# Two-layer graph network: row halves for even and odd bodies in layer one, and in layer two one pick fewer and one gather more in one group of every fourth body

## The chip, the cores and the metric

The kernel runs on one core of one Trainium2 chip. The metric is the time of one execution on the device in microseconds (us), as the median of several executions. TensorE is called PE here (PEld is its weight load), VectorE DVE, ScalarE ACT, GpSimd POOL, SyncE SP.

## The reference, cut to what matters

Two layers of message passing over 6250 nodes with 64 features and 200,000 edges that are sorted by their target `dst`:

```python
# x: (6250, 64)   src, dst: (200000,)   edge_attr: (200000, 64)   edge_weight: (200000,)
h = maximum(layernorm(x), 0)
y = h @ W0 + b0                                            # layer one
agg = segment_sum(edge_weight[:, None] * y[src], dst, 6250)
deg = segment_sum(edge_weight, dst, 6250)
x = x + relu(agg / (deg[:, None] + 1e-6))

h = maximum(layernorm(x), 0)                               # layer two
m = gelu(concat([h[src], edge_attr]) @ W_msg + b_msg)
g = (1 + eps) * h + segment_sum(m, dst, 6250)
out = x + gelu(g @ W_upd + b_upd)
```

Each layer needs, for every edge, the row of a 6250 x 64 table at the edge's source, and adds up what it makes of it by the edge's target.

## The kernel before, in words

**Tiling.** The edges are cut into groups of 1024 (G = 128 x J, J = 8 tiles of 128 edges). There are 196 groups. Four groups (SLOTS = 4) make a body, so there are 49 bodies (BODIES) in each layer. Every engine has its own program, written out by hand in order, with loops (`Fori`) whose passes are bodies; the engines keep step by counting semaphores alone. There is no planner.

**Layer one.** Of the 8 tiles of a group, JA (4 or 5, by zone) are treated as products with small adjacency blocks on PE (`blocks_of`, L940; `adjacency_sums`, L959), and the other JH = J - JA (3 or 4) by gathered rows: POOL issues one indirect DMA per tile (`gathers`, L628 to L641) that fetches 128 rows of the table `h0_table` into `rows[:, slot, j, :]`, by the indices in `idx[:, slot, j]`. ACT's `weigh` (L764) waits for the rows of a slot, copies the next body's eight indices into `idx` (`copy_idx`, L670), and writes the weighted rows to `wrows` (L771), which counts up `s_used[slot]`. POOL gathers for the same slot of the next body only once that has happened. DVE builds the one-hot tiles (`build`, L1406 and L1408), and PE adds up by target in windows of 72 nodes (`window`, L1000). The five zones have different block shapes; the loops of a zone cover the bodies whose next two bodies lie in the same zone, and the bodies at a zone's edge are written out singly (`STRETCHES`). PE's loops of layer one are made with `hint_back_edge=True`.

**Between the layers** the sums are turned into the second table `p1_table`. `all_rounds` (on PE and DVE, ahead of the last body of layer one) holds the code for targets that lie too far apart; it is jumped over when there are none.

**Layer two.** Of the 8 tiles of a group, six (J0) are gathered from `p1_table` by POOL, and the last two (PICKS = 2) are "picked" on PE: the table lies in SBUF as `parts` (two parts of 7 x 448 columns), DVE compares the sources with the node number and makes a 0/1 matrix (`make_pick`, L1452), PE multiplies it with `parts` (`picks`, L917 to L934, the matmuls at L930: 2 tiles x 7 x 2 = 28 of 128x448 per group), and DVE masks out and adds up the right one of seven column blocks (`picked_rows`, L1469 and L1473) into `rows[:, slot, 6:8, :]`. PE also transposes the edge features (L1124), multiplies them by the lower half of W_msg (`edge_product`, L1135). DVE adds that product and the rows (`message_sum`, L1675; it waits for the slot's gathers, and counts up `s_used`), ACT applies the gelu (L860), and PE adds up by target in windows (L1000), two groups at a time; DVE adds these to the node sums (`sums`, L1490, and a small memset, L1510, that marks a group as done). If a group's targets span more than one window, `more_windows` (PE) and its counterpart in `sums` (DVE) do further ones; their code lies in the loop, and is jumped over otherwise.

PE's and DVE's order is one group ahead: in step s of a body, PE transposes and picks for group s + 1, then does the windows of groups s - 1 and s (for odd s), and then the product of group s + 1. The loops on PE, DVE, ACT and POOL run over 48 bodies, one body a pass, and the last body follows singly. PE's loop of layer two has no hint.

Of the kernel before, what the change touches and what calls it, by code (L numbers as in the profile page):

```python
# [7 lines left out]
class Zone:  # L8
# [43 lines left out]
    def gathered(self, b):  # L52
        return b * self.JH + (self.gathers_before - self.first * self.JH)


def two_layer_gnn(
# [97 lines left out]
    assert ZONES[-1].end == BODIES  # L154
    JA = max(z.JA for z in ZONES)
# [29 lines left out]
    GATHERED = ZONES[-1].gathered(BODIES)  # L185
    BANKS = (3, 5)
# [15 lines left out]
    with ctx:  # L202
# [235 lines left out]
        s_gat = [sem(f"gathered{s}") for s in range(SLOTS)]  # L438
# [24 lines left out]

        def unit(t, u):

            return t[:, u * KB:(u + 1) * KB, :]
# [10 lines left out]
        def _(sp):  # L477


            for one in (*s_used, s_prow, s_sumTc, s_sumc):  # L480
                sp.sem_inc(one, 1)
            sp.sem_inc(s_block, RING)
# [123 lines left out]
        @block.gpsimd  # L606
        def _(pool):
            nc.gpsimd.memset(ident[:, :], 0.0).then_inc(s_identf, 1)
            pool.wait_ge(s_identf, 1)
            nc.gpsimd.affine_select(out=ident[:, :], in_=ident[:, :], compare_op=ALU.not_equal, fill=1.0,  # L610
                                    base=0, pattern=[[-1, P]], channel_multiplier=1).then_inc(s_const, 1)
            nc.gpsimd.iota(iota_i[:, :], pattern=[[1, KH * P]], base=0, channel_multiplier=0).then_inc(s_const, 1)
            nc.gpsimd.memset(rows[:, :, :, D:DA], 1.0).then_inc(s_const, 1)
            nc.gpsimd.iota(node_i[:, :], pattern=[[0, 1]], base=0,
                           channel_multiplier=1).then_inc(s_const, 1)

            pool.wait_ge(s_src, 64)
            nc.gpsimd.tensor_copy(src_f[:, 0, :], src_raw[:, 0, :])
            nc.gpsimd.tensor_copy(src_f[0:HALF[1], 1, :], src_raw[0:HALF[1], 1, :]).then_inc(s_srcf, 1)
            pool.wait_ge(s_dst, 64)  # L620
            nc.gpsimd.tensor_copy(dst_f[:, 0, :], dst_raw[:, 0, :])
            nc.gpsimd.tensor_copy(dst_f[0:HALF[1], 1, :], dst_raw[0:HALF[1], 1, :]).then_inc(s_dstf, 1)
            nc.gpsimd.memset(sums_sb[:, :], 0.0).then_inc(s_zero, 1)
            for layer, table in ((0, h0_table), (1, p1_table)):
                if layer == 1:
                    pool.wait_ge(s_agg, UNITS)
                    nc.gpsimd.memset(sums_sb[D:DA, :], 0.0).then_inc(s_cleared, 1)
                pool.wait_ge(s_tabw[layer], (UNITS + 1) * 16)  # L628

# [13 lines left out]

                if layer == 0:
                    for z in ZONES:
                        with pool.Fori(z.first + 1, z.end + 1) as turn:
                            gathers(turn, range(z.JA, J))
                else:
                    with pool.Fori(BODIES + 1, 2 * BODIES) as turn:
                        gathers(turn, range(J0))  # L650
                    gathers(2 * BODIES, range(J0))

        @block.scalar
        def _(act):
# [53 lines left out]
            for s in range(SLOTS):  # L708
                copy_idx(s, s)
# [54 lines left out]
            def weigh(z, b, s, next_g):  # L764

                act.wait_ge(s_gat[s], z.gathered(b) * 16 + 16 * z.JH)
                copy_idx(next_g, s)
                act.wait_ge(s_dw[0], b * SLOTS + (s + 1))
                act.wait_ge(s_done, b * SLOTS + (s + 1))
                for j in range(z.JH):  # L770
                    last = nc.scalar.activation(wrows[s][:, j, :], rows[:, s, z.JA + j, :], ACT.Copy,  # L771
                                                scale=dw[:, s, 1, j:j + 1])
# [7 lines left out]
            def first(b, here, ahead, further):  # L780

                for s in range(2):
                    weigh(here, b, s, (b + 1) * SLOTS + s if ahead else s)
# [6 lines left out]
                for s in range(2, SLOTS):  # L790
                    weigh(here, b, s, (b + 1) * SLOTS + s if ahead else s)
# [61 lines left out]
            def message(b, s):  # L853
# [4 lines left out]
                act.wait_ge(s_used[s], b + (1 + BODIES + 1))  # L858
# [22 lines left out]
        def _(pe):  # L881
# [36 lines left out]
            def picks(b, q):  # L918
# [7 lines left out]
                for t in range(PICKS):  # L926
# [117 lines left out]
            def first(b, here, ahead, further):  # L1044
# [6 lines left out]
                for s in range(1, SLOTS, 2):  # L1051
# [6 lines left out]
                    for r in (s - 1, s):  # L1058
                        if not ahead and r == SLOTS - 1:
                            busy(28)  # L1060
                        pe.wait_ge(s_used[r], b + 2)
# [66 lines left out]
            def edge_product(b, s, shift):  # L1128
# [3 lines left out]
                if shift:  # L1132
                    pe.wait_ge(s_used[s], b + (1 + BODIES + 1))
# [10 lines left out]
            def second(b, last_body):  # L1144
                for s in range(SLOTS):
                    if not (last_body and s == SLOTS - 1):
                        edge_transpose(b, s, 1)
                        picks(b, s + 1)
# [32 lines left out]
        def _(dve):  # L1181
# [279 lines left out]
            def picked_rows(b, q):  # L1461
# [4 lines left out]
                dve.wait_ge(s_used[q % SLOTS], b + (BODIES + q // SLOTS + 1))  # L1466
                dve.wait_ge(s_prow, g + 1)
                of = mask[:, bass.ds(g, 1), :, :].rearrange("p g t a -> p (g t) a")
                nc.vector.tensor_tensor(sel[:, :, :, :],  # L1469
                                        ps[:, bank:bank + PICKS, 0:NA * D].rearrange("p t (a d) -> p t a d", d=D),  # L1470
                                        of.unsqueeze(3).to_broadcast([P, PICKS, NA, D]), ALU.mult).then_inc(s_sel, 1)
                dve.wait_ge(s_sel, g + 1)
                nc.vector.tensor_reduce(rows[:, q % SLOTS, J0:J, 0:D],  # L1473
                                        sel[:, :, :, :].rearrange("p t a d -> p t d a"),
# [191 lines left out]
            def message_sum(b, s, shift):  # L1666
# [4 lines left out]
                dve.wait_ge(s_gat[slot], 16 * GATHERED  # L1671
                            + (b + (s + shift) // SLOTS + 1) * (16 * J0))
# [9 lines left out]
            def second(b, last_body):  # L1682
                for s in range(SLOTS):
# [8 lines left out]
                    if not (last_body and s == SLOTS - 1):  # L1692
                        picked_rows(b, s + 1)
                        message_sum(b, s, 1)
# [45 lines left out]
```

## Time and profile before

| what | value |
|---|---|
| three runs | 2615.12, 2619.41, 2618.65 us, median 2618.65 |
| the profiled execution | 2620.69 us, its span 2618.9 us |
| PE busy | 2437.3 us (93%), 21749 matmuls |
| PEld busy | 2273.1 us (87%) |
| DVE busy | 2012.4 us (77%) |
| ACT busy | 1560.6 us (60%) |
| POOL busy | 1791.4 us (68%), 1879 instructions |
| layer one | from the start to about 1034 us |
| layer two's first picks | at 1077 us |

The span goes from the first to the last instruction. Each row of a timeline has the start, the duration, the engine, the line of the kernel, the operation with its operands, and in brackets the idle time of the engine just before it and what ended that ("issue": nothing that the profile shows). A busy PE is not PE at its peak, since the ends of matmuls are modelled. The share of a whole span is an average over two layers with different limits, so the windows of one stage say more than the page's first part.

### The profile page before, as it was taken

How to read it: one execution, taken by the hardware profiler on the slowest of the kernel's cores; microseconds unless marked ns; L12 is line 12 of the kernel's file. 1: busy time of each engine (PE TensorE's matmuls, PEld its weight loads, DVE VectorE, ACT ScalarE, POOL GpSimd, SP SyncE). 2: the span in 40 equal slices, each digit the busy share in tenths (PEclk: the TensorE clock that was granted, in tenths of full speed). 3: DMA queues.
4: the chain of work that ended last, by engine and by line, in shares of the span. 5: the costliest groups of instructions: out<-in, count | busy, mean ns of one | idle time of the engine just before them, and what ended most of it. 6: DMA issues, size and time to landing. Idle time of an engine off the chain costs nothing.

```text
span 2618.9 us, 70760 instructions
## 1 busy us (share of the span) xinstructions
PE 2437.3 (93%) x21749; PEld 2273.1 (87%) x21750; DVE 2012.4 (77%) x4216; ACT 1560.6 (60%) x5144; POOL 1791.4 (68%) x1879
## 2 busy tenths in 40 slices
PE   1588899999888888899999999999999999999998
PEld 1477799999888888899999999999999999999998
DVE  7888887766888886777777777777777777777774
ACT  2466666665666664566555656665656566556653
POOL 3377765677777773477777777777777777777771
PEclk9999999999999998899999999999999999999997
DMA  6111111111111110344444444445454544445451
GB/s 117 38 26 27 25 24 21 25 26 26 26 25 24 25 25 22 86 122 119 120 119 121 118 122 118 122 118 125 116 121 120 121 119 119 119 120 120 118 121 37
DMA packets 472280, 213.80 MB, mean 82 GB/s; under 512 B 264668, under 2 KB 441656, under 8 KB 472196
## 3 DMA queue, kind: packets, MB, share of 16 engines
q1 hardware_dynamic: 412548, 151.55, 22.1%
q0 software_dynamic: 59648, 61.20, 12.8%
q8 instruction: 45, 0.74, 0.1%
q14 instruction: 39, 0.32, 0.0%
HBM read 207.09 MB, written 5.51 MB: 81 GB/s over the span
## 4 chain that ended last, share of the span: by engine, by line
PE 58%; DVE 0%; ACT 0%; issue 0%; DVEq 0%
PE ps L930 43%; PE ps L1135 7%; PE ps L1000 4%; PE ps L1124 3%; PE ps L1082 1%; PE ps L1029 0%; DVE rows L1473 0%; DVE parts L1231 0%; DVE sel L1469 0%; DVE room L1675 0%; ACT h_sb L860 0%; DVE h_sb L1706 0%; DVE h_sb L1711 0%; ACT h_sb L878 0%; DVE tick L1510 0%
## 5 line engine op out<-in xcount | busy, mean ns | idle before, releaser
L639 POOL DMA_INDIRECT rows<-p_table,idx x1176 | 1109.8, 944 | 390.0 <-issue 342.8
L930 PE MATMUL ps<-parts,pick_all 128*128 128x448 f32 x5488 | 1162.0, 369 | 2.6 <-DVE parts L1231 2.6
L930 PEld LDWEIGHTS ps<-parts,pick_all 128*128 128x128 f32 x5488 | 1019.4, 189 | 77.7 <-issue 2.9
L639 POOL DMA_INDIRECT rows<-h_table,idx x688 | 665.3, 967 | 324.3 <-issue 200.9
L940 PE MATMUL ps<-hot_c,hot_p 128*128 128x150 f32 (+4 forms) x2336 | 435.0, 313 | 64.9 <-issue 37.1
L1469 DVE TENSOR_TENSOR sel<-ps,mask 128x896 f32<-128x896 f32 x196 | 214.0, 1092 | 307.0 <-PE ps L930 298.3
L940 PEld LDWEIGHTS ps<-hot_c,hot_p 128*128 128x128 f32 x2336 | 371.7, 192 | 85.7 <-issue 63.8
L731 ACT COPY adj<-ps 128x500 f32<-128x500 f32 (+4 forms) x880 | 349.9, 448 | 149.5 <-PE ps L940 136.9
L1452 DVE TENSOR_SCALAR pick_all<-src_all,node_f 128x1792 fp32r<-128x1792 int16 x196 | 406.5, 2074 | 27.4 <-issue 24.7
L1406 DVE TENSOR_SCALAR hot_p<-iota_p,scal 128x128 f32<-128x128 f32 (+2 forms) x880 | 301.1, 342 | 76.5 <-PE ps L940 56.0
L1473 DVE TENSOR_REDUCE rows<-sel 128x128 f32<-128x896 f32 x196 | 342.7, 1749 | 6.7
L1408 DVE TENSOR_SCALAR hot_c<-iota_c,scal 128x250 fp32r<-128x250 f32 (+4 forms) x880 | 340.8, 387 | 0.0
L860 ACT ACTIVATE h_sb<-room 128x512 f32<-128x512 f32 x98 | 62.0, 633 | 352.4 <-DVE room L1675 352.4
L959 PE MATMUL ps<-adj,h_sb 128*64 128x160 f32 (+4 forms) x4802 | 260.9, 267 | 1.9 <-ACT adj L731 0.9
L959 PEld LDWEIGHTS ps<-adj,h_sb 128*64 128x64 f32 x4802 | 250.4, 137 | 6.9 <-issue 2.0
L1000 PEld LDWEIGHTS ps<-onehot,room 128*65 128x65 f32 (+1 forms) x3336 | 175.1, 138 | 76.1 <-issue 59.0
L1000 PE MATMUL ps<-onehot,room 128*65 128x72 f32 (+1 forms) x3336 | 190.1, 229 | 50.8 <-DVE room L1447 41.9
L1135 PE MATMUL ps<-W1b_sb,eT 128*128 128x128 f32 x1568 | 216.6, 281 | 0.0
L1135 PEld LDWEIGHTS ps<-W1b_sb,eT 128*128 128x128 f32 x1568 | 197.5, 191 | 10.1
L860 ACT ACTIVATE room<-room 128x512 f32<-128x512 f32 x98 | 62.0, 632 | 240.8 <-DVE room L1675 240.8
L754 ACT ACTIVATE h_sb<-iota,dw 128x72 f32<-128x72 f32 x784 | 203.5, 345 | 0.0
L754 ACT ACTIVATE onehot<-iota,dw 128x72 f32<-128x72 f32 x784 | 203.3, 344 | 0.0
(182 smaller groups left out, 2345.0 us busy)
## 6 DMA issues: line engine op xcount, KB each, us to landing
src_all<-keys SPq DMA_DIRECT2D x196, 448.0 KB
ea<-in_edge_attr_dram SPq DMA_DIRECT2D x196, 256.0 KB
rows<-p_table,idx POOLq DMA_INDIRECT x1176
rows<-h_table,idx POOLq DMA_INDIRECT x688
x_sb<-in_x_dram SPq DMA_DIRECT2D x6, 224.0 KB, 4.3
h_table<-h_sb SPq DMA_DIRECT2D x6, 224.0 KB
p_table<-h_sb SPq DMA_DIRECT2D x6, 224.0 KB
out_dram<-h_sb SPq DMA_DIRECT2D x6, 224.0 KB
```

Source lines behind the costliest of these rows:

```text
L639: nc.gpsimd.indirect_dma_start(out=rows[:, s, j, 0:D], out_offset=None, in_=table[:, :], in_offset=bass.IndirectOffsetOnAxis(ap=idx[:, s, ...
L731: nc.scalar.copy(adj[:, 0:z.KH * z.KW, t * z.WT:(t + 1) * z.WT], psA[t % BANKS1][:, 0:z.KH * z.KW * z.WT].rearrange("p (k w) -> p k w", w= ...
L754: last = nc.scalar.activation(hots[s][:, j, :], iota[:, :], ACT.Abs, scale=-1.0, bias=dw[:, s, 0, j:j + 1])
L930: last = nc.tensor.matmul(to, hot[:, k, t * P:(t + 1) * P], parts[:, part, k, :, :].rearrange("p a d -> p (a d)"), start=(k == 0 and part ...
L940: last = nc.tensor.matmul(to[:, k * z.KW * z.WT:(k + 1) * z.KW * z.WT], one[:, k * P:(k + 1) * P], two[i], start=(i == 0), stop=(i == z.WP ...
L959: last = nc.tensor.matmul(psX[h:h + D, 0:z.cols], h_sb[:, n, :], adj[:, n, 0:z.cols], start=(n < 2), stop=(n >= NB - 2))
L1000: last = nc.tensor.matmul(psW[s % 2][at:at + width, :], lhs(j), hot[:, j, :], start=(j < sets), stop=(j >= n - sets))
L1135: last = nc.tensor.matmul(psM[:, q * P:(q + 1) * P], eT[:, q * P:(q + 1) * P], W1b_sb[:, :], start=True, stop=True)
L1406: nc.vector.tensor_scalar(one, iota_p[:, 0:z.KH * P], number(0), None, ALU.is_equal)
L1408: last = nc.vector.tensor_scalar(two[i], iota_c[:, 0:z.KW * z.WT], number(1), number(2 + i), ALU.is_equal, ALU.mult)
L1452: nc.vector.tensor_scalar(pick_all[:, q % 2, :].rearrange("p (k e) -> p k e", k=KA), src_bc[:, q % 2, :, 0:PICKS * P], node_f[:, 0:1], Non ...
L1473: nc.vector.tensor_reduce(rows[:, q % SLOTS, J0:J, 0:D], sel[:, :, :, :].rearrange("p t a d -> p t d a"), AX.X, ALU.add).then_inc(s_prow, 1)
```

## The change

In layer one each slot of `rows` and `idx` is used as two halves of four tiles (SET = 4), one for even and one for odd bodies, with semaphores `s_gat` of their own. POOL may then gather for a body as soon as the body two before it has been weighed (`s_used` starts at 2 instead of 1). ACT copies only the indices that are gathered, and for two bodies ahead; POOL's and ACT's loops of layer one make two bodies a pass.

In layer two the loops on POOL, PE and DVE make four bodies a pass (LOOP = 4), 12 passes instead of 48. In the last group (slot 3) of the fourth body, the first of the two picked tiles is gathered instead (`one_pick`): PE makes 14 of the 28 matmuls there, DVE masks and adds one tile instead of two, POOL issues seven gathers instead of six, and the count for which `message_sum` waits on that slot grows by one with each pass. ACT's loop of layer two stays at one body a pass.

```diff
+    def gathered_half(self, h):
+        return h * self.JH + (self.gathers_before // 2 - self.first // 2 * self.JH)
...
+    SET = J // 2
...
+    LOOP = 4
...
-        s_gat = [sem(f"gathered{s}") for s in range(SLOTS)]
+        s_gat = [[sem(f"gathered{p}_{s}") for s in range(SLOTS)] for p in range(2)]
...
+        def one_pick(phase, slot):
+
+            return phase == LOOP - 1 and slot == SLOTS - 1
...
+            for one in s_used:
+                sp.sem_inc(one, 2)
...
-                def gathers(turn, tiles):
+                def gathers(turn, free, tiles, p, phase=0):
                     for s in range(SLOTS):
                         pool.wait_ge(s_const, CONSTS)
                         pool.wait_ge(s_idx[s], turn)
 
-                        pool.wait_ge(s_used[s], turn)
+                        pool.wait_ge(s_used[s], free)
                         if s == 0:
                             pool.sem_inc(s_passed, 1)
-                        for j in tiles:
+                        for j in range(tiles.start, tiles.stop + one_pick(phase, s)):
                             nc.gpsimd.indirect_dma_start(
...
-                            ).then_inc(s_gat[s], 16)
+                            ).then_inc(s_gat[p][s], 16)
+
+                def half_gathers(z, b, p):
+                    gathers(b + 1, b + 1, range(p * SET, p * SET + z.JH), p)
 
                 if layer == 0:
                     for z in ZONES:
-                        with pool.Fori(z.first + 1, z.end + 1) as turn:
-                            gathers(turn, range(z.JA, J))
+                        with pool.Fori(z.first // 2, z.end // 2) as h:
+                            for p in range(2):
+                                half_gathers(z, 2 * h + p, p)
+                        if z.end % 2:
+                            half_gathers(z, z.end - 1, 0)
                 else:
-                    with pool.Fori(BODIES + 1, 2 * BODIES) as turn:
-                        gathers(turn, range(J0))
-                    gathers(2 * BODIES, range(J0))
+                    with pool.Fori(0, (BODIES - 1) // LOOP) as i:
+                        for phase in range(LOOP):
+                            turn = i * LOOP + (BODIES + 1 + phase)
+                            gathers(turn, turn + 1, range(J0), 0, phase)
+                    gathers(2 * BODIES, 2 * BODIES + 1, range(J0), 0)
...
+            def copy_half_idx(z, b, p, s):
+                nc.scalar.copy(idx[:, s, p * SET:p * SET + z.JH].unsqueeze(2),
+                               src_tab[:, z.JA:J, bass.ds(b * SLOTS + s, 1)]).then_inc(s_idx[s], 1)
...
-            for s in range(SLOTS):
-                copy_idx(s, s)
+            for p in range(2):
+                for s in range(SLOTS):
+                    copy_half_idx(ZONES[0], p, p, s)
...
-            def weigh(z, b, s, next_g):
-
-                act.wait_ge(s_gat[s], z.gathered(b) * 16 + 16 * z.JH)
-                copy_idx(next_g, s)
+            def weigh(z, b, h, p, s, ahead, further):
+
+                act.wait_ge(s_gat[p][s], z.gathered_half(h) * 16 + 16 * z.JH)
+                if further:
+                    copy_half_idx(further, b + 2, p, s)
+                elif not ahead:
+                    copy_idx(s, s)
...
-                    with act.Fori(start, end) as b:
-                        first(b, *zones)
-                else:
-                    first(start, *zones)
+                    with act.Fori(start // 2, end // 2) as h:
+                        for p in range(2):
+                            first(2 * h + p, h, p, *zones)
+                if (end - start) % 2:
+                    first(end - 1, (end - 1) // 2, (end - 1) % 2, *zones)
...
-                for t in range(PICKS):
+                for t in range(one_pick(phase, q), PICKS):
                     to = ps[:, BANKS[q % 2] + t, 0:NA * D]
...
-            with pe.Fori(0, BODIES - 1) as b:
-                second(b, False)
-            second(BODIES - 1, True)
+            with pe.Fori(0, (BODIES - 1) // LOOP) as i:
+                for phase in range(LOOP):
+                    second(i * LOOP + phase, phase, False)
+            second(BODIES - 1, 0, True)
...
+                own = slice(int(one_pick(phase, q)), PICKS)
+                n = PICKS - own.start
+                of = mask[:, bass.ds(g, 1), own, :].rearrange("p g t a -> p (g t) a")
...
-                dve.wait_ge(s_gat[slot], 16 * GATHERED
-                            + (b + (s + shift) // SLOTS + 1) * (16 * J0))
+                landed = 16 * GATHERED + (b + (s + shift) // SLOTS + 1) * (16 * J0)
+                if slot == SLOTS - 1:
+
+                    landed = landed + (i + one_pick(phase, slot)) * 16
+                dve.wait_ge(s_gat[0][slot], landed)
...
-            with dve.Fori(0, BODIES - 1) as b:
-                second(b, False)
-            second(BODIES - 1, True)
+            with dve.Fori(0, (BODIES - 1) // LOOP) as i:
+                for phase in range(LOOP):
+                    second(i * LOOP + phase, phase, False, i)
+            second(BODIES - 1, 0, True, (BODIES - 1) // LOOP)
```

## Rows read from the trace of the kernel before

**Rows 1.** The page's chain that ended last, share of the span by engine.
```profile
PE 58%; DVE 0%; ACT 0%; issue 0%; DVEq 0%
```

**Rows 2.** Windows, layer two: length, busy us (instructions) by engine, granted PE clock, DMA.
```profile
1200.00:2500.00 1300.00, 1300.00 (x9500) 1201.45 (x9499) 979.52 (x1015) 786.51 (x2283) 970.87 (x1030) 1.00 0.49 120
```

**Rows 3.** Chain of waits, layer two: start, us, what; two picks, two groups apart.
```profile
1516.90 5.67 PE ps L930 x28
...
1532.25 5.67 PE ps L930 x28
```

**Rows 4.** Timeline of POOL, layer two: first, 12th, 18th, 606th and last gather.
```profile
1078.43 0.95 POOL L639 DMA_INDIRECT rows<-p_table,idx  x1 [14.88 <-issue]
...
1092.17 0.94 POOL L639 DMA_INDIRECT rows<-p_table,idx  x1 [0.30 <-issue]
...
1099.66 0.94 POOL L639 DMA_INDIRECT rows<-p_table,idx  x1 [0.30 <-issue]
...
1833.74 0.94 POOL L639 DMA_INDIRECT rows<-p_table,idx  x1 [0.30 <-DVE room L1675]
...
2562.41 0.95 POOL L639 DMA_INDIRECT rows<-p_table,idx  x1 [0.30 <-issue]
```

**Rows 5.** L639: one wait of POOL before it (us, times); who waited for it.
```profile
  ACT room L771: 123.4, 52
...
  DVE room L1675: 2.3, 1
```

**Rows 6.** Timeline of DVE, layer two: message sums, and a body's end and next start.
```profile
1096.07 0.69 DVE L1675 TENSOR_TENSOR room<-ps,rows 128x512 f32<-128x512 f32 x1
...
1105.13 0.69 DVE L1675 TENSOR_TENSOR room<-ps,rows 128x512 f32<-128x512 f32 x1 [2.30 <-DMA rows<-p_table,idx]
...
1518.79 0.06 DVE L1510 MEMSET tick<- 1x1 f32 x1
1519.37 2.08 DVE L1452 TENSOR_SCALAR pick_all<-src_all,node_f 128x1792 fp32r<-128x1792 int16 x1 [0.52 <-issue]
...
2584.56 0.69 DVE L1675 TENSOR_TENSOR room<-ps,rows 128x512 f32<-128x512 f32 x1 [0.20 <-DVE rows L1473]
```

**Rows 7.** The page's queues that fetch instructions: packets, MB, share of 16 engines.
```profile
q8 instruction: 45, 0.74, 0.1%
q14 instruction: 39, 0.32, 0.0%
```

**Rows 8.** Timelines of PE and DVE, layer one: idle times without a semaphore, and 661.49.
```profile
632.70 3.65 PE L940 MATMUL ps<-hot_c,hot_p 128*128 128x200 f32 x12 [2.39 <-issue]
...
661.49 1.47 PE L1000 MATMUL ps<-onehot,room 128*65 128x72 f32 x20 [2.74 <-DVE room L1447]
...
997.30 0.37 PE L940 MATMUL ps<-hot_c,hot_p 128*128 128x250 f32 x1 [2.85 <-issue]
...
1014.60 0.53 DVE L1400 TENSOR_TENSOR onehot<-iota,dw 128x360 f32<-128x360 f32 x1 [3.98 <-issue]
...
1021.26 0.28 PE L970 MATMUL ps<-eye,xs 128*40 128x64 f32 x2 [3.61 <-issue]
```

**Rows 9.** Timeline of PE around the jump from one body of layer two to the next.
```profile
1514.16 1.22 PE L1000 MATMUL ps<-h_sb 128*64 128x72 f32 x32
1515.31 1.16 PE L1135 MATMUL ps<-W1b_sb,eT 128*128 128x128 f32 x8
...
1516.66 5.92 PE L930 MATMUL ps<-parts,pick_all 128*128 128x448 f32 x28
...
1523.66 5.92 PE L930 MATMUL ps<-parts,pick_all 128*128 128x448 f32 x28
```

**Rows 10.** Windows around three of the idle times of rows 8; the clock is third last.
```profile
632.00:640.00 8.00, 7.30 (x46) 7.01 (x46) 4.38 (x14) 3.06 (x7) 5.71 (x6) 0.79 0.14 29
661.00:669.00 8.00, 6.88 (x72) 6.43 (x72) 7.24 (x25) 5.50 (x20) 5.79 (x7) 1.00 0.12 23
997.00:1001.00 4.00, 3.69 (x19) 3.51 (x20) 2.58 (x9) 1.86 (x4) 3.05 (x4) 0.57 0.15 31
```

More of the change, by code:

```diff
@@ L154, in two_layer_gnn @@
     assert ZONES[-1].end == BODIES
+    SET = J // 2
+    assert all(z.JH <= SET and z.first % 2 == 0 and z.gathers_before % 2 == 0 for z in ZONES)
     JA = max(z.JA for z in ZONES)
@@ L184, in two_layer_gnn @@
     J0 = J - PICKS
-    GATHERED = ZONES[-1].gathered(BODIES)
-    BANKS = (3, 5)
+    LOOP = 4
+    assert (BODIES - 1) % LOOP == 0
+    GATHERED = ZONES[-1].gathered_half((BODIES + 1) // 2)
     BANKS = (3, 5)
@@ L477, in _ @@
         def _(sp):
-            for one in (*s_used, s_prow, s_sumTc, s_sumc):
+            for one in (s_prow, s_sumTc, s_sumc):
                 sp.sem_inc(one, 1)
+            for one in s_used:
+                sp.sem_inc(one, 2)
             sp.sem_inc(s_block, RING)
@@ L770, in weigh @@
                 for j in range(z.JH):
-                    last = nc.scalar.activation(wrows[s][:, j, :], rows[:, s, z.JA + j, :], ACT.Copy,
+                    last = nc.scalar.activation(wrows[s][:, j, :], rows[:, s, p * SET + j, :], ACT.Copy,
                                                 scale=dw[:, s, 1, j:j + 1])
@@ L778, in next_dw, with first @@
                 copy_dw(0, b * SLOTS + s, s % SLOTS, z)
-            def first(b, here, ahead, further):
+            def first(b, h, p, here, ahead, further):
                 for s in range(2):
-                    weigh(here, b, s, (b + 1) * SLOTS + s if ahead else s)
+                    weigh(here, b, h, p, s, ahead, further)
                 for s in range(2, SLOTS):
@@ L790, in first @@
                 for s in range(2, SLOTS):
-                    weigh(here, b, s, (b + 1) * SLOTS + s if ahead else s)
+                    weigh(here, b, h, p, s, ahead, further)
                     if ahead:
@@ L916, in _, with picks @@
                 turn(w_raw, half, psR[half])
-            def picks(b, q):
+            def picks(b, q, phase=0):
                 hot = pick_all[:, q % 2, :].rearrange("p (k e) -> p k e", k=KA)
@@ L1142, in _, with second @@
             edge_product(0, 0, 0)
-            def second(b, last_body):
+            def second(b, phase, last_body):
                 for s in range(SLOTS):
@@ L1147, in second @@
                         edge_transpose(b, s, 1)
-                        picks(b, s + 1)
+                        picks(b, s + 1, phase)
                     last_group = last_body and s == SLOTS - 1
@@ L1459, in next_pick, with picked_rows @@
                 make_pick(b, q)
-            def picked_rows(b, q):
+            def picked_rows(b, q, phase=0):
                 g = b * SLOTS + q
@@ L1465, in picked_rows @@
                 dve.wait_ge(s_picked, g + 1)
-                dve.wait_ge(s_used[q % SLOTS], b + (BODIES + q // SLOTS + 1))
+                dve.wait_ge(s_used[q % SLOTS], b + (BODIES + q // SLOTS + 2))
                 dve.wait_ge(s_prow, g + 1)
[L1468 to L1471, printed above, removed]
+                own = slice(int(one_pick(phase, q)), PICKS)
+                n = PICKS - own.start
+                of = mask[:, bass.ds(g, 1), own, :].rearrange("p g t a -> p (g t) a")
+                nc.vector.tensor_tensor(sel[:, own, :, :],
+                                        ps[:, bank + own.start:bank + PICKS, 0:NA * D].rearrange(
+                                            "p t (a d) -> p t a d", d=D),
+                                        of.unsqueeze(3).to_broadcast([P, n, NA, D]), ALU.mult).then_inc(s_sel, 1)
                 dve.wait_ge(s_sel, g + 1)
-                nc.vector.tensor_reduce(rows[:, q % SLOTS, J0:J, 0:D],
-                                        sel[:, :, :, :].rearrange("p t a d -> p t d a"),
+                nc.vector.tensor_reduce(rows[:, q % SLOTS, J0 + own.start:J, 0:D],
+                                        sel[:, own, :, :].rearrange("p t a d -> p t d a"),
                                         AX.X, ALU.add).then_inc(s_prow, 1)
@@ L1680, in _, with second @@
             message_sum(0, 0, 0)
-            def second(b, last_body):
+            def second(b, phase, last_body, i):
                 for s in range(SLOTS):
@@ L1692, in second @@
                     if not (last_body and s == SLOTS - 1):
-                        picked_rows(b, s + 1)
-                        message_sum(b, s, 1)
+                        picked_rows(b, s + 1, phase)
+                        message_sum(b, s, 1, phase, i)
                     if s % 2:
```

8 lines of the change are left out of this document (4 added, 4 removed).

## The prediction

> **What bounds the kernel now.** I read the page's chain of waits first: PE alone holds 58% of the span in it and no other engine a whole per cent [rows 1]. The windows then say where: from 1200 to 2500 us PE is busy 1300.00 of 1300.00 us, DVE 980, POOL 971, ACT 787, at a granted clock of 1.00 [rows 2]. So layer two is a pure PE chain, and what comes off PE there comes off the end, as long as nothing else steps into its place. The pieces of that chain are the picks: 28 matmuls in 5.67 us, and every two groups take 15.35 us (1516.90 to 1532.25) [rows 3], so a body of four takes 30.70.
>
> The page's busy share (POOL 68%) misleads about what stands next. From 1078.43 to 1833.74 POOL issues 606 gathers back to back, one in 755.31 / 605 = 1.248 us (0.94 busy and 0.30 between) [rows 4]. A body's 24 take 29.96 us, so POOL is only 0.74 us a body faster than PE. It starts late and needs some 25 bodies to catch up; only then does it wait for free slots.
>
> Layer one is another matter: POOL waits 123.4 us there for ACT's weighing, but nothing waits for a gather of layer one; the one engine held up by a gather is DVE, once, 2.3 us, in layer two [rows 5].
>
> **The change part by part.** The profiled execution took 2620.69 us with a span of 2618.9; the median of the three runs is 2618.65, 2.04 less. I work out differences on the profiled one and put them on the median.
>
> *Halves of the slots in layer one.* It removes waits of POOL (a gather for body b+1 no longer needs body b weighed). Since no engine waits for those gathers [rows 5], I take 0. It costs four more index copies ahead of the loops, where ACT goes on to wait for DVE's and PE's tables (that wait hides them; without it, under a microsecond), and 12 gathers earlier there; bound: a microsecond or two either way. ACT's loops become two bodies long. No new instruction stands on PE.
>
> *One pick fewer.* 14 matmuls at 5.67 / 28 = 0.2025 us are 2.84 us [rows 3], in 12 groups: 34.0 us off PE's chain. DVE's multiply and sum of these groups halve; DVE has 320 us to spare in the 1300 [rows 2], so that is worth nothing.
>
> *One gather more.* 12 x 1.248 = 15.0 us more on POOL. Per four bodies POOL needs 97 x 1.248 = 121.1 us, PE 4 x 30.70 - 2.84 = 119.9: POOL would be the slower one by 1.2 us a pass and never catch up. The end that POOL allows: the last of 1188 gathers ends at 1078.43 + 1187 x 1.2485 + 0.95 = 2561.3. From there to landing, two rows bound it: the message sum at 1105.13 waited for a gather issued by 1100.60 (4.53 us), the one at 1096.07 did not wait on one issued by 1093.11 (at most 2.96) [rows 4, 6]. So the last message sum, now at 2584.56 [rows 6], can't come before 2564.3 to 2565.8: of the 34.0 us no more than 18.8 to 20.3, say 19.5, can be had. What follows that sum stays as it is. Behind the added gather stand only POOL's own next gathers, and the first to be held up by them is that message sum.
>
> The Trainium skill (DMA: Bandwidth & Descriptors, Anatomy of one DMA, SWDGE path) gives about 2.0 us of fixed cost to such a transfer; the row with 4.53 us disagrees for at least one gather, and by the page's figure the cap would be an estimated 21.3 us.
>
> *Four bodies of code in one pass.* This is the part I give most weight. PE's and DVE's loops of layer two now hold four bodies, and PE's loop has no hint for its jump back. A pass today runs 9500 matmuls and 9499 weight loads in 1300 us, about 448 records in 30.70 us, and PE never stalls at the jump [rows 2]. The instruction queues fetched 45 and 39 packets in the whole span [rows 7]; one packet per pass of this loop would already be 48. So one body's code stays at hand. Whether four bodies' code does, no row shows. What code that is not at hand costs, rows do show, as idle time with no semaphore behind it ("issue"): at the first matmuls after a loop of layer one is left, 2.39 us (632.70) and 2.85 us (997.30); after the jump over the further rounds, PE 3.61 us (1021.26) and DVE 3.98 us (1014.60), where DVE's usual gap at a jump back is 0.52 (1519.37) [rows 6, 8].
>
> There are 12 passes, so 11 jumps back. Bounds of the price on PE: 0 and 3.61 us each. I take (2.39 + 2.85) / 2 = 2.62, the rows that stand at a loop's end on PE. At the jump back PE has little queued: after the last product of a body (1515.31 to 1516.47) come the next transposes and picks (1516.66) [rows 9].
>
> A stall of that size can also bring PE's granted clock from its upper level (2.4 GHz) to its lower (1.2): around the 2.39 us idle the granted clock of 8 us was 0.79 (lost 0.21 x 8 = 1.7 us), around the 2.85 us idle that of 4 us 0.57 (0.43 x 4 = 1.7 us), but around an idle of 2.74 us 1.00 (nothing) [rows 8, 10]. I take two passes of three at 1.7 us: 1.1 us a pass. Bounds: 0 and 1.7. Nothing hides either: PE is the chain [rows 1, 2].
>
> DVE's own jump: 3.98 - 0.52 = 3.46 us later, its pick would be ready at 1521.45 + 3.46 = 1524.91, and PE wants it at 1523.66 [rows 6, 9]: 1.25 us late if PE is on time, nothing if PE itself stalls 2.62. So it does not add.
>
> *Sum.* -34.0 + 11 x (2.62 + 1.13) = -34.0 + 41.3 = +7.3 us. POOL's cap does not bind: a pass of PE is 123.7 us against POOL's 121.1. 2618.65 + 7.3 = 2626.
>
> The Trainium skill (Runtime: NRT & Kernel Launch, Instruction fetch mechanics) says that code is held in blocks of 256 instructions, 2048 of them on PE and 512 on the others, that straight code is fetched ahead, and that a taken branch to code outside the window waits for the fetch. Its other sentence, of only two such blocks, the trace contradicts for PE: 448 records, the skipped branch's products (another 32 matmuls and as many loads a group pair, by the row at 1514.16 [rows 9]) and the waits are more than 512, and no pass stalls. By the 2048, one body fits, and four, at least 4 x (448 + 128) = 2304 by my estimate, do not, so the stall would come in every pass.
>
> **Rivals.**
> 1. *No stall at the jump back; POOL becomes the bound* (the other side: faster). The four bodies stay at hand, or the queue covers the fetch. For it: 48 jumps back today without a stall; against it: code four times as long as any shown to be kept. PE would end 34.0 us earlier, POOL allows 19.5: 2599. It holds as long as the stall is under (34.0 - 19.5) / 11 = 1.3 us a pass; a stall of DVE alone (1.25 us) ends here too.
> 2. *Stall, but the clock holds.* For it: the 2.74 us idle; against it the two others. -34.0 + 11 x 2.62 = -5.2: 2613.
> 3. *Stall at its upper row, clock down each time.* 11 x (3.61 + 1.7) = 58.4, less 34.0: +24.4, 2643. For it: the far jump's 3.61 is also a taken branch, while the loop ends are not.
> 4. *The earlier gathers of layer one matter.* No engine waits for them; a microsecond or two, inside every range.
>
> **How the numbers follow.** A measurement of this kernel tells 0.2%, 5.2 us, from no change. Forecast case 0.52, own range 2617 (2.39 a pass and the clock down in one of three: 11 x 2.96 - 34.0 = -1.4) to 2635 (2.85 and down in all: 11 x 4.55 - 34.0 = +16.1); rival 1 0.28; rival 2 0.10; rival 3 0.10. Faster: 0.28, half of rival 2 (0.05) and 0.03 of the forecast: 0.36. Same: the other half of rival 2 and 0.17 of the forecast: 0.22. Slower: 0.32 of the forecast and rival 3: 0.42. The range for 8 in 10 has to reach rival 1 and rival 3: 2598 to 2645.
>
> **What would show it.** In the windows, PE's busy time in layer two: 100% less 2.6 us every 122 us or so if I am right, with 11 idle times marked "issue" ahead of the transposes (L1124), a granted clock under 1.00 there, and some hundred more instruction packets. Rival 1 shows the packets nearly unchanged or the idle under 1.3 us, POOL back to back (1.248 us) until the end, and DVE's message sum waiting for gathers. Picks: 12 groups with 14 matmuls in 2.84 us; L930 falls from 5488 to 5320. POOL's layer-one wait for L771 should shrink while layer one ends where it does. I am wrong if PE's idle at the passes is small, if layer one's end moves by more than 3 us, or if a gather takes another time than 1.248 us.

## The result and the profile after

The changed kernel takes 2653.6 us (median of 4 runs), the kernel before in the same comparison 2616.9: a ratio of 1.0157, 95% interval 1.0124 to 1.019. It is slower by about 1.6%, where the prediction said 2626 (+7.3 us) with a range up to 2645. The profiled execution has a span of 2657.3 us, 38.4 more than the one before.

Where the 38.4 lie, the first and last picks of layer two say. In the timeline of PE of the kernel before they are:

```profile
1077.46 8.37 PE L930 MATMUL ps<-parts,pick_all 128*128 128x448 f32 x28 [2.64 <-DVE parts L1231]
...
2575.58 5.92 PE L930 MATMUL ps<-parts,pick_all 128*128 128x448 f32 x28
```

and in that of the changed kernel (the picks' line is now L959):

```profile
1075.67 7.98 PE L959 MATMUL ps<-parts,pick_all 128*128 128x448 f32 x28 [2.19 <-DVE parts L1261]
...
2613.96 5.92 PE L959 MATMUL ps<-parts,pick_all 128*128 128x448 f32 x28
```

From the start of the first to the end of the last, layer two took 2581.50 - 1077.46 = 1504.04 us before and 2619.88 - 1075.67 = 1544.21 after: +40.2, with 168 matmuls fewer. Layer one and the way into layer two took 1.8 us less, the tail the same (37.4 us each). The 1.8 is chance as far as the traces show: the twelve kernels of the experiments have the layer one of the changed kernel, and there the first picks start anywhere from 1070.7 to 1082.7. I call this stretch "layer two" below and compare kernels by it; the three kernels with all picks in which PE never stands there agree within 1 us (1503.2 to 1504.2).

The window that stood in [rows 2], the instruction queues of [rows 7], and PE's and DVE's waits in layer two, all of the changed kernel:

```profile
1200.00:2500.00 1300.00, 1250.23 (x9024) 1149.59 (x9023) 931.53 (x983) 762.21 (x2214) 949.61 (x1007) 0.98 0.49 118
```

```profile
q8 instruction: 184, 3.01, 0.5%
q14 instruction: 124, 1.02, 0.1%
```

```profile
PE ps L1153 <- issue: 48.4, 11, 6.2
...
DVE pick_all L1482 <- issue: 37.6, 22, 3.5
...
DVE room L1711 <- DMA rows<-p_table,idx: 10.6, 4, 5.1
```

PE was never idle in this window before; now it is for 50 us of it, and over all of layer two it stands 48.4 us at 11 places, all ahead of the transposes that open a pass (L1153, the old L1124), with no semaphore to blame. The instruction packets on q8 rose from 45 to 184: (184 - 45) / 11 = 12.6 a jump at most, since the first pass through the longer code has its packets in the 184 too.

One such place, in the timelines of PE and then of DVE of the changed kernel; the brackets hold the idle time before the row and what ended it:

```profile
1448.17 3.08 PE L959 MATMUL ps<-parts,pick_all 128*128 128x448 f32 x14
1451.09 1.05 PE L1164 MATMUL ps<-W1b_sb,eT 128*128 128x128 f32 x8
1451.98 0.60 PE L1153 MATMUL ps<-ident,ea 128*128 128x128 f32 x4
1452.68 6.04 PE L959 MATMUL ps<-parts,pick_all 128*128 128x448 f32 x28
...
1459.80 1.16 PE L1164 MATMUL ps<-W1b_sb,eT 128*128 128x128 f32 x8
1465.43 0.72 PE L1153 MATMUL ps<-ident,ea 128*128 128x128 f32 x4 [4.47 <-issue]
1465.84 7.49 PE L959 MATMUL ps<-parts,pick_all 128*128 128x448 f32 x28
1473.17 1.05 PE L1164 MATMUL ps<-W1b_sb,eT 128*128 128x128 f32 x8
1474.06 0.60 PE L1153 MATMUL ps<-ident,ea 128*128 128x128 f32 x4
1474.41 5.92 PE L959 MATMUL ps<-parts,pick_all 128*128 128x448 f32 x28
```

```profile
1450.55 2.08 DVE L1482 TENSOR_SCALAR pick_all<-src_all,node_f 128x1792 fp32r<-128x1792 int16 x1
...
1463.22 0.06 DVE L1543 MEMSET tick<- 1x1 f32 x1
1466.53 2.08 DVE L1482 TENSOR_SCALAR pick_all<-src_all,node_f 128x1792 fp32r<-128x1792 int16 x1 [3.26 <-issue]
```

Three losses are to be read here. PE stands 4.47 us at the jump. Its next 28 picks, from the transposes' start to the product's (1465.43 to 1473.17), take 7.74 us. Undisturbed it is 5.95 from the end of one product to the next (1516.47 [rows 9] to 1522.42 in the kernel before, below, where the transposes start 0.16 us before that end). Of the 1.79 us more, 0.16 is this lost overlap and the rest the clock. And after the thinner group (14 matmuls, 1448.17) the next picks begin 0.70 us after their transposes (1451.98, 1452.68), where 0.35 is usual (1474.06, 1474.41), because DVE made the pick for them only from 1450.55 to 1452.63. That recurs behind all 12 thinner groups. The two rows of the kernel before:

```profile
1516.31 0.60 PE L1124 MATMUL ps<-ident,ea 128*128 128x128 f32 x4
...
1522.42 1.05 PE L1135 MATMUL ps<-W1b_sb,eT 128*128 128x128 f32 x8
```

The windows of the changed kernel show the clock (third column from the right):

```profile
1461.00:1465.00 4.00, 0.00 (x0) 1.00 0.23 35
1465.00:1469.00 4.00, 3.57 (x13) 0.61 0.45 96
1469.00:1473.00 4.00, 4.00 (x21) 0.96 0.52 147
1473.00:1477.00 4.00, 4.00 (x27) 1.00 0.34 76
```

### The profile page after: what moved, and what is told of

Its sections match the earlier page's. It is cut to its first block, busy times and chain, and to the rows that moved or that the text cites. A ratio compares the mean times of both kernels' runs of the same rounds, so it can differ in the third digit from the quotient of the medians.

```text
span 2657.3 us, 69927 instructions
## 1 busy us (share of the span) xinstructions
PE 2427.3 (91%) x21581; PEld 2258.4 (85%) x21582; DVE 1993.3 (75%) x4216; ACT 1560.9 (59%) x5144; POOL 1805.8 (68%) x1891
## 4 chain that ended last, share of the span: by engine, by line
PE 66%; DVE 18%; issue 8%; POOL 3%; DVEq 3%; DMA 1%; ACT 1%; SPq 0%; POOLq 0%; ACTq 0%
PE ps L959 37%; PE ps L969 8%; PE ps L1029 6%; PE ps L1164 6%; PE ps L988 5%; DVE hot_c L1438 5%; DVE hot_p L1436 4%; POOL rows L651 3%; PE ps L1153 3%; DVE hot_lo L1438 2%; DVEq L1515 1%; DVE pick_all L1482 1%; PE ps L1111 1%; DVE rows L1506 1%; DVE sums_sb L1523 1%
## 5 line engine op out<-in xcount | busy, mean ns | idle before, releaser
L959 PE MATMUL ps<-parts,pick_all 128*128 128x448 f32 x5320 | 1144.4, 373 | 3.5 <-DVE parts L1261 2.2
L959 PEld LDWEIGHTS ps<-parts,pick_all 128*128 128x128 f32 x5320 | 1001.2, 191 | 82.0 <-DVE pick_all L1482 4.1
L1501 DVE TENSOR_TENSOR sel<-ps,mask 128x896 f32<-128x896 f32 x196 | 208.2, 1062 | 335.3 <-PE ps L959 327.0
L1482 DVE TENSOR_SCALAR pick_all<-src_all,node_f 128x1792 fp32r<-128x1792 int16 x196 | 406.5, 2074 | 43.8 <-issue 37.6
L1506 DVE TENSOR_REDUCE rows<-sel 128x128 f32<-128x896 f32 x196 | 332.1, 1695 | 6.7
```

Of the source, the lines that this page charges most:

```text
L959: last = nc.tensor.matmul(to, hot[:, k, t * P:(t + 1) * P], parts[:, part, k, :, :].rearrange("p a d -> p (a d)"), start=(k == 0 and part ...
L1482: nc.vector.tensor_scalar(pick_all[:, q % 2, :].rearrange("p (k e) -> p k e", k=KA), src_bc[:, q % 2, :, 0:PICKS * P], node_f[:, 0:1], Non ...
L1506: nc.vector.tensor_reduce(rows[:, q % SLOTS, J0 + own.start:J, 0:D], sel[:, own, :, :].rearrange("p t a d -> p t d a"), AX.X, ALU.add).the ...
```

## The experiments

My theory F: PE's loop of four bodies is more code than stays at hand, so that PE waits at every jump back and then runs at the lower clock. Rival D: PE's gap is a wait for DVE, which stands at its own jump. Rival P: the thinner groups and added gathers cost the time. Layer two lasts, in us, with PE's idle at the jumps and the ratio of the whole time to the kernel before:

| kernel | layer two | PE's idle, waits | ratio (95%) |
| --- | --- | --- | --- |
| before | 1504.0 | 0 | 1 |
| changed | 1544.2 | 48.4, 11 for code | 1.0157 (1.0124 to 1.019) |
| halves alone | 1503.2 | 0 | 0.9986 (0.9961 to 1.0011) |
| four bodies of code, no thinner group | 1581.6 | 50.2, 11 for code | 1.0263 (1.0214 to 1.0312) |
| four on PE alone | 1580.9 | 50.0, 11 for code | 1.0268 (1.0219 to 1.0318) |
| four on DVE alone | 1510.7 | 2.9, 9 for picks | 1.0000 (0.998 to 1.0019) |
| three bodies of code | 1571.4 | 45.4, 15 for code | 1.0225 (1.0186 to 1.0263) |
| two bodies of code | 1530.0 | 19.5, 23 for picks | 1.0102 (1.0061 to 1.0143) |
| two on PE alone | 1504.2 | 0 | 1.0009 (0.9987 to 1.0031) |
| changed, hint on PE | 1516.9 | 29.8, 11 for code | 1.0075 (1.0046 to 1.0105) |
| nest of four | 1493.6 | 13.2, 11 for picks | 0.9961 (0.9937 to 0.9986) |
| nest of six | 1496.8 | 8.1, 7 for picks | 0.9956 (0.9932 to 0.998) |
| nest of four, hint on DVE | 1483.3 | 0.4, 1 for a pick | 0.9942 (0.9921 to 0.9962) |
| nest of six, hint on DVE | 1488.4 | 0 | 0.9972 (0.9954 to 0.999) |

### The parts of the change alone

Halves alone. All picks are put back and the loops of layer two hold one body:

```diff
-            return phase == LOOP - 1 and slot == SLOTS - 1
+            return False
...
-            with pe.Fori(0, (BODIES - 1) // LOOP) as i:
+            with pe.Fori(0, (BODIES - 1) // 1) as i:
```

(the loops of DVE and POOL likewise; with no thinner group, `message_sum` no longer adds the passes to its count).

> Layer one's halves alone: loops of one body in layer two, all picks put back. Both theories: no stall on PE, 2615 us (layer two begins 1.8 us earlier than in the kernel before: 1075.67 against 1077.46), instruction packets on q8 about 45. If the halves themselves cost something in layer two (by an earlier state of POOL or by ACT's longer code), over 2620.

2604.97 us against 2609.28 in its comparison: no difference that can be told, and PE is busy through the window again:

```profile
1200.00:2500.00 1300.00, 1300.00 (x9499) 1200.60 (x9498) 977.51 (x1018) 789.11 (x2293) 972.85 (x1030) 1.00 0.50 120
```

Four bodies of code with all picks put back:

```diff
-            return phase == LOOP - 1 and slot == SLOTS - 1
+            return False
```

(`message_sum` is changed as above)

> The changed kernel with all picks put back (28 matmuls in each group, 24 gathers a body), loops of four bodies kept. Theory F: the loss stands alone, 2617 - 1.8 (layer two begins that much earlier) + 11 x (4.4 + 1.8) = 2683 us, slower than the changed kernel. Rival P (the added gathers and the thinner groups cost the time, the idle is only where it shows): about 2615, as before.

2682.31 us. The expected 2683 came from F's prices in the changed kernel, and P fell: without a thinner group or an added gather the kernel is slower still.

Four bodies on PE alone, against the kernel just named:

```diff
-            with dve.Fori(0, (BODIES - 1) // LOOP) as i:
+            with dve.Fori(0, (BODIES - 1) // 1) as i:
...
-                    with pool.Fori(0, (BODIES - 1) // LOOP) as i:
+                    with pool.Fori(0, (BODIES - 1) // 1) as i:
```

> As the kernel with halves alone, but PE's loop of layer two holds four bodies; DVE's and POOL's hold one. Theory F: all of the loss is PE's own, 2683 us, PE's idle 4.4 us at 11 jumps though DVE never stands at its own; q8 about 184 packets, q14 as before. Theory D: 2615.

2683.21 us. The page's queues and the wait, with DVE's packets back at the 44 of the halves alone:

```profile
q8 instruction: 184, 3.01, 0.5%
q14 instruction: 44, 0.36, 0.0%
```

```profile
PE ps L1153 <- issue: 50.0, 11, 5.1
```

DVE did not stand at its jumps here, and PE's idle is the same: D is out, the loss is PE's own code. Layer two is 77.7 us longer than with the halves alone, 50.0 of it idle and 26.5 the slower picks behind the 11 jumps (counted as above, with 0.16 a jump of lost overlap).

Four bodies on DVE alone, against the same kernel of four bodies:

```diff
-            with pe.Fori(0, (BODIES - 1) // LOOP) as i:
+            with pe.Fori(0, (BODIES - 1) // 1) as i:
...
-                    with pool.Fori(0, (BODIES - 1) // LOOP) as i:
+                    with pool.Fori(0, (BODIES - 1) // 1) as i:
```

> As the kernel with halves alone, but only DVE's loop of layer two holds four bodies; PE's and POOL's hold one. DVE alone is to pay: about 3.5 us idle at 11 jumps, its pick then some 0.9 to 1.2 us late for PE (as in the loops of two, 19.5 us in 23 waits), 11 x 1.0 = 10 to 13 us: ratio to the kernel before about 1.003 to 1.005, q8 45 packets, q14 about 44 + 11 x 7.3 = 124. If DVE's stall is hidden when PE is on time, 1.000.

The ratio says no difference; the profile says 7.5 us more in layer two than with the halves alone (0.7 a jump, 11 jumps), less than expected:

```profile
q14 instruction: 124, 1.02, 0.1%
```

```profile
PE ps L959 <- DVE pick_all L1482: 2.9, 9, 0.5
```

Only q14 rose here (q8 stays at 45), and only q8 with four bodies on PE alone: q8 carries PE's code, q14 DVE's.

### How much code stays at hand

Loops of three bodies, of two, and of two on PE alone with one on DVE and POOL, all without a thinner group; on PE

```diff
-            with pe.Fori(0, (BODIES - 1) // LOOP) as i:
-                for phase in range(LOOP):
-                    second(i * LOOP + phase, phase, False)
+            with pe.Fori(0, (BODIES - 1) // 3) as i:
+                for phase in range(3):
+                    second(i * 3 + phase, phase, False)
```

(and with 2 for 3):

> As the kernel with halves alone, loops of three bodies: 9.5 packets of PE's code a pass, 15 jumps. Theory F1 with the amount below 9.5 packets: 15 x (4.55 + 2.2) = +100, 2707 us, q8 about 45 + 15 x 9.5 = 185. F1 with the amount above it: 2605 to 2609, q8 near 45. A partial loss (only the blocks that do not fit are fetched anew) would lie between, with fewer than 185 packets.

> As the kernel with halves alone (all picks put back), but the loops of layer two hold two bodies on PE, DVE and POOL. In the loop of four PE took (184 - 45) / 11 = 12.6 instruction packets a pass, about 3.2 a body. Theory F1 (PE keeps a fixed amount of code; a loop within it is fetched once, one beyond it is fetched anew in every pass): two bodies are 6.3 packets; if that is within the amount, no idle at the jumps, q8 near 45 packets, 2605 to 2609 us. Theory F2 (any loop much longer than one body is fetched anew): 23 jumps x (4.4 + 1.8) = +143, 2750 us.

> As the kernel with halves alone, but only PE's loop holds two bodies. If what the loops of two cost (19.5 us of PE waiting for DVE's pick) is all DVE's, this costs nothing: ratio 0.998 to 1.001, q8 47 packets, q14 44, no wait of PE. If PE's longer code costs by itself, some 20 us, 1.008.

Three bodies: 2673.5 us. PE fetches (94 - 45) / 15 = 3.3 packets a jump at most and stands 3.03 us at each. That is the partial loss which the expectation named last, not the full refetch.

```profile
q8 instruction: 94, 1.54, 0.2%
```

```profile
PE ps L1153 <- issue: 45.4, 15, 3.4
```

Two bodies: PE's packets stay at 47 and it never waits for code, but it waits for DVE's pick, which is late because DVE now stands at its jump; the time is 2638.1 us against 2618.2. Neither theory had said so. The page's queues, PE's wait, and one of DVE's jumps:

```profile
q14 instruction: 160, 1.31, 0.2%
q8 instruction: 47, 0.77, 0.1%
```

```profile
PE ps L959 <- DVE pick_all L1482: 19.5, 23, 1.2
```

```profile
1337.51 2.08 DVE L1482 TENSOR_SCALAR pick_all<-src_all,node_f 128x1792 fp32r<-128x1792 int16 x1 [3.66 <-issue]
```

With two on PE alone (q8 47, q14 44) layer two lasts 1504.2: on PE two bodies are free, and the two-body cost was DVE's.

The 3.2 packets a body in these expectations (6.3 for two, 9.5 for three) are too many. A kernel with a loop of two has one more copy of the body than one with a loop of one, and where nothing is fetched again q8 rises by it from 45 to 47 (the nests below, with as many copies, have 47 too): 2 packets a copy, under 3 in any case. With 2 each for the added copies the refetches are (94 - 49) / 15 = 3.0 a jump for three bodies and (184 - 51) / 11 = 12.1 for four, which is as much as all four bodies or more.

### Undoing the stall

The hint for the jump back, which PE's loops of layer one have, on PE's loop of layer two in the changed kernel:

```diff
-            with pe.Fori(0, (BODIES - 1) // LOOP) as i:
+            with nc.Fori(0, (BODIES - 1) // LOOP, engines=(mybir.EngineType.PE,), hint_back_edge=True) as i:
```

> The changed kernel whole; the one edit is the hint for the jump back on PE's loop of layer two (the same hint that PE's loop of layer one has). Theory F (PE waits at each of its 11 jumps for its own code, 4.40 us, and then runs at the lower clock, 1.8 us): if the hint has the loop's first code there in time, both go, 11 x 6.2 = 68 us less on PE, and POOL becomes the bound: 2597 us, up to 2610 if DVE's own idle at its jump (3.3 us) now shows by 1.25 us each time; PE's idle ahead of the transposes under 1 us. If the hint brings only the loop's first block and the rest is still fetched late, the idle shrinks to half, about 2625. Theory D (PE's gap is a wait for DVE, which stands 3.3 us at its own jump): nothing changes, 2653, since DVE has no hint.

2631.61 us against 2609.28: still slower than before, near the middle case (2625). Layer two is 27.3 us shorter than in the changed kernel: 18.6 of idle, 9.1 of slower picks. The page's packets and PE's wait:

```profile
q8 instruction: 174, 2.85, 0.5%
```

```profile
PE ps L1153 <- issue: 29.8, 11, 3.8
```

The packets fell by about one a jump, and the idle time from 4.41 to 2.71 us. That fits a hint that brings only the start of the loop early, while the rest is still fetched anew; the trace does not show which packet is which.

The nest keeps the work of the change with two bodies of code: an inner loop makes one body three times, and the fourth, with the thinner group, is written out behind it (on DVE and POOL as on PE; the nest of six has 6 for 4):

```diff
-            with pe.Fori(0, (BODIES - 1) // LOOP) as i:
-                for phase in range(LOOP):
-                    second(i * LOOP + phase, phase, False)
+            with pe.Fori(0, (BODIES - 1) // 4) as i:
+                with pe.Fori(0, 4 - 1) as k:
+                    second(i * 4 + k, 0, False)
+                second(i * 4 + (4 - 1), LOOP - 1, False)
```

> The work of the changed kernel (halves, one pick fewer and one gather more in every fourth body), but each pass of four is an inner loop of one body, three times, and a fourth body written out: two bodies of code on PE, DVE and POOL. Theory F1 with room for two bodies: no stall on PE, 12 x (2.84 - 0.35) = 29.9 us off PE, POOL (97 gathers of 1.248 us a pass, 121.1 us) is the bound; the cap of the prediction, 19 to 21 us below the kernel before: 2588 to 2590. If leaving the inner loop and entering it again stalls as leaving a loop did in layer one (2.4 to 2.85 us), the 12 exits cost 29 to 34 us and nothing is gained: about 2610.

> The same nest with the thinner group in every sixth body, 8 in all. PE: 8 x (2.84 - 0.35) = 19.9 us less; POOL: 145 gathers, 181.0 us a pass against PE's 181.7, so POOL's cap (24.5 us) does not bind: 2588 us by F1 with room for two bodies, no better than the nest of four, but with POOL off the path.

Both beat the kernel before: 2607.2 and 2600.6 us against 2618.2, and PE stands for code once, 0.6 us. The full gain is missing because DVE stands some 4.2 us at the outer jump (3.6 to 4.6; at 8 of the 11 the trace names PE's picks as the releaser, but with the hint below all 11 go). In the nest of four (the picks' line is L961 in the nests):

```profile
PE ps L961 <- DVE pick_all L1485: 13.2, 11, 3.0
```

So the last two kernels hint DVE's outer loop:

```diff
-            with dve.Fori(0, (BODIES - 1) // 4) as i:
+            with nc.Fori(0, (BODIES - 1) // 4, engines=(mybir.EngineType.DVE,), hint_back_edge=True) as i:
```

> The nest of four with the hint on the outer jump back of DVE's loop alone. In the nest without it DVE stands about 4.2 us idle at 11 outer jumps and PE waits 13.2 us for its pick. If the hint brings DVE's code in time, PE's wait falls to about 4 us (0.35 a pass is left behind the thinner group); POOL, back to back to the end in the nest, allows 8 to 9.5 us (last gather over at 2554.9, last message sum at 2567.4, 3 to 4.5 us for landing): 8 us under the nest of four, ratio to the kernel before 0.993, and POOL the bound: the last message sums wait for gathers. If the hint shortens DVE's idle only by a third, as PE's did from 4.4 to 2.7, DVE's pick is still just in time (its lead without a stall is about 2.2 us): the same. If the hint does nothing on DVE: 0.996 as the nest.

> The nest of six with the same hint. PE's wait falls from 8.1 us to 2 or 3; POOL is not the bound: 5 to 6 us under the nest of six, ratio 0.993 to 0.994, the same as the nest of four with the hint.

The nest of four with the hint takes 2601.6 us against 2616.8. That is the best ratio here, though its interval overlaps those of the two nests without the hint. DVE's waits, PE's, and POOL's last gather beside DVE's last message sum:

```profile
PE ps L961 <- DVE pick_all L1485: 0.4, 1, 0.4
...
DVE room L1714 <- DMA rows<-p_table,idx: 40.8, 41, 3.3
```

```profile
2561.24 0.94 POOL L651 DMA_INDIRECT rows<-p_table,idx  x1 [0.30 <-issue]
```

```profile
2564.38 0.69 DVE L1714 TENSOR_TENSOR room<-ps,rows 128x512 f32<-128x512 f32 x1 [0.20 <-DVE rows L1509]
```

Layer two is 20.7 us shorter than before, PE waits for no pick but one, and DVE's message sums wait for gathers 41 times, three of the last five among them. POOL issues all 1188 gathers back to back and is at its cap. PE is still busy for 1446.4 of the 1450 us from 1100 to 2550, so the two end nearly together, and that POOL alone is the bound is not shown. DVE's packets on q14 are 45, one more than with one body: the hint on DVE took away the refetch too, not only the wait. The nest of six with the hint (2606.6) was no equal of it, against the expectation. Its layer two is 8.4 us shorter than without the hint, but the ratio did not improve. In both hinted nests DVE stands 2.7 to 2.9 us within the last body, ahead of the memset that marks a group (L1546; 0.4 without the hint), and PE's first update waits 3.2 to 3.4 us for it. That gives part back, and the clock gives back more: behind this wait the tail ran at 0.50 in both hinted nests (40.5 and 40.2 us from the last pick's end), while both nests without the hint had it at 1.00 (25.8 us each).

## Why the prediction was wrong

The place and the mechanism were as forecast; the two sizes that price it were too small.

| term | predicted | measured |
| --- | --- | --- |
| 168 picks fewer | -34.0 | -34.0 (12 groups, 2.84 each) |
| idle at 11 jumps | 11 x 2.62 = 28.8 | 48.4 (4.41 each) |
| clock behind them | 11 x 1.13 = 12.4 | 20.8 (1.72 to 2.67 each, 0.16 of it lost overlap) |
| DVE's pick behind the thinner group | 0 | 12 x 0.35 = 4.2 |
| layer one | 0 | -1.8, by chance |
| sum | +7.3 | +37.6, of 38.4 by the spans |

**The step that failed** is the price of a stall at the jump: "I take (2.39 + 2.85) / 2 = 2.62, the rows that stand at a loop's end on PE"; 4.41 was measured. A loop's end goes straight on. The loop's jump back is taken, and of the rows in hand the far jump's 3.61 us [rows 8] was of that kind. I had even noted this for rival 3, and then priced it at a tenth of the chances. That the kind of row is what made 2.62 too small is my reading. The amount fetched again counts as well: the jump of three bodies, also taken, cost 3.03. Even 3.61 was not the upper bound that I called it: 9 of 11 jumps of the changed kernel cost 4.1 us or more, the two least 3.94 and 3.97.

**The clock** came down behind all 11 jumps, not two of three, and cost up to 2.67 us each, above the 1.7 of [rows 10] (0.16 of each is the lost overlap). With the hint the idle times were shorter, 2.3 to 3.0 us after the first, and the picks behind were slow by over 1.6 us in 5 passes of 11 and by 0.32 in the other six. In the loop of three (2.7 to 3.4 us) it was 9 of 15. So my two of three is not far from what these shorter idle times show (14 of 26 in the two kernels); behind the longer ones of the changed kernel it was every one. What decides in the middle is not the idle time alone: 2.35 us was followed by the slow picks, 2.96 was not.

**What was not in the sum** is DVE's pick behind the thinner group. I looked for DVE's slack as a share of 1300 us. A group that is 2.84 us shorter on PE is also asked of DVE 2.84 us earlier, and there DVE had 2.84 - 0.35 = 2.5 to spare.

**What held.** The halves of layer one are worth nothing that can be told, though POOL's wait for the weighing fell from 123.4 us [rows 5] to 96.1. DVE's own longer loop does not add to PE's: alone it cost 0.7 us a pass, I had said 1.25. POOL's cap, 18.8 to 20.3 us, bound nothing in the changed kernel but showed in the nest of four with the hint: layer two is 20.7 us shorter, and its last message sum starts at 2564.38, where I had 2564.3 as the earliest. That sum began 2.2 us after the last gather was issued and did not wait on it, so landing took less than the 2.96 and 4.53 that bounded it. The Trainium skill (DMA: Bandwidth & Descriptors, Anatomy of one DMA, SWDGE path) has about 2.0, and this row is consistent with it.

The Trainium skill (Runtime: NRT & Kernel Launch, Instruction fetch mechanics) puts PE's store at 2048 instructions in blocks of 256. A packet of q8 is 0.74 MB / 45 = 16 KB; by the Trainium skill the store would be eight such blocks. The runs agree in part. At 2 packets a body, under 3, two bodies take 4 (under 6) and stay, and four take 8 (under 12) and are fetched again in every pass. But three take 6 (under 9), which may lie on either side of eight, and lose a part: the store's size is not measured here. The Trainium skill gives no price for the taken branch; here it is 4.4 us at four bodies and 3.0 at three.

The first idle time, 6.25 us, is longer than the rest. DVE's longest wait for a gather (5.08 us) ends in the same microsecond, at 1211.08, and in the loops of four without the thinner group the first idle time is like the others (4.51 and 4.53). But the message sum that had waited ended at 1211.77, after PE had gone on at 1211.50, so it was not what released PE; the cause stays open.

## What to carry to other kernels

Before the loop of the engine that bounds the kernel is made longer, read its code in instruction packets: if a pass of the longer loop fetches packets again, each jump costs several microseconds and often the clock as well (here 6.3 us), as much as some thirty saved matmuls. Price a jump back by rows of jumps that fetch their code, and treat the largest row as a sample and not as a bound. A rare variant of a body belongs behind an inner loop of the common one, so that two bodies of code do the work of four. Then look at every engine's loop, not at the bounding one alone.

## What the runs showed of the hardware

The update behind layer two runs at either of the two clock levels, and that alone moves the whole time by some 12 us. Windows of PE in that tail, of the kernel before and of the halves alone (busy us, granted clock):

```profile
2597.00:2605.00 8.00, 8.00 (x42) 0.50 0.29 73
```

```profile
2587.00:2591.00 4.00, 4.00 (x41) 1.00 0.46 115
```

From the last pick's end to the end of the span it is 2618.9 - 2581.5 = 37.4 us at 0.50 and 2601.3 - 2575.8 = 25.5 at 1.00, with the same two short waits ahead of it (1.27 and 0.59 us before, 1.3 and 0.6 there). Why one execution falls to the lower level and another does not is not shown. A single pair of times of this kernel is therefore worth little below half a per cent (the 0.2% of the prediction was too fine), which is why layer two was compared by its own stretch. The nest of four with the hint:

```profile
2580.00:2590.00 10.00, 10.00 (x54) 0.50 0.24 58
```

Its nine executions all took 2597.8 to 2605.4 us, without the wide spread of the nest without the hint (2592.0 to 2614.5). That fits a tail at the lower level every time, behind the 3.4 us wait, but only one of the nine was traced.

On DVE the hinted nest took 45 packets in all, so it fetched nothing again. A loop of two bodies without the hint fetched (160 - 45) / 23 = 5.0 packets a jump, and the nest of two bodies without it (100 - 45) / 11 = 5.0 too. So two bodies can stay on DVE, and yet are fetched again when the jump is not announced; why stays open.
